# A graph layer whose sender rows come by indirect gather: one tile of 32 fetched row by row from two hardware queues

## The reference

```
h   = relu(layernorm(x))
s,v = h[:, :32] @ W_up_s, h[:, 32:] as [n, 32, 3] @ W_up_v      # the node table
w0..w3 = split(silu(silu(ef @ A1 + b1) @ A2 + b2) @ A3)          # per edge, ef has 8 features
ss, vs = s[src], v[src]                                         # one table row of 128 per edge
messages = [ss*y_s*w0, <vs,y_v>*w3/sqrt3, ss*y_v*w1, vs*y_s*w2] # 256 per edge
sums = segment_sum(messages, dst) / 10
out  = x + sums @ (W_out_s, W_out_v)
```

## Time and profile before

| | |
|---|---|
| profiled execution | 2015.58 us, span 2013.8 us |
| median of 3 runs | 2017.62 us |
| GpSimd busy | 1490.8 us (74%); 1563 gathers of 944 ns, 475.7 us of issue between them |
| TensorE busy | 1534.8 us (76%), mean granted clock 0.857 |
| VectorE busy | 977.2 us (49%) |
| ScalarE busy | 417.8 us (21%) |
| DMA engines | about 2 tenths busy in each slice, mean 64 GB/s |

### The profile page before, as it was taken

How to read it: one execution, slowest core, us unless ns; L and a number is a source line. 1 busy time by engine, 2 the same in 40 slices (tenths; PEclk the granted TensorE clock), 3 DMA queues, 4 the chain that set the end, 5 groups by cost and what they waited for, 6 DMA issues and landing times.

```text
span 2013.8 us, 47824 instructions
## 1 busy us (share of the span) xinstructions
PE 1534.8 (76%) x16198; PEld 936.5 (47%) x16198; DVE 977.2 (49%) x2232; ACT 417.8 (21%) x836; POOL 1490.8 (74%) x1627
## 2 busy tenths in 40 slices
PE   6877878778788787787787877777868777778685
PEld 3544545445444444454444444544545445444443
DVE  4444444444444444444444444444444444444444
ACT  4222222222222222222222222222222222212221
POOL 4777777777777777777777777777777777777774
PEclk8888898888978988879888888898898888988987
DMA  8222222222222222222222222222222222222222
GB/s 231 58 60 58 59 57 60 57 59 58 59 57 60 57 59 58 59 59 58 59 57 60 57 59 58 59 57 60 57 59 58 59 57 60 57 59 58 59 57 101
DMA packets 110964, 128.22 MB, mean 64 GB/s; under 512 B 70498, under 2 KB 83074, under 8 KB 110820
## 3 DMA queue, kind: packets, MB, share of 16 engines
q0 software_dynamic: 50336, 102.64, 18.1%
q1 hardware_dynamic: 60420, 25.36, 4.7%
q10 hardware_dynamic: 192, 0.02, 0.0%
HBM read 121.46 MB, written 6.43 MB: 64 GB/s over the span
## 4 chain that ended last, share of the span: by engine, by line
POOL 71%; issue 25%; POOLq 1%; PE 0%; DMA 0%; DVE 0%; SPq 0%; ACT 0%; DVEq 0%
POOL rows L520 71%; POOLq L515 1%; POOLq L517 0%; POOLq L525 0%; DMA rows<-node_table,src_in 0%; PE pss L740 0%; PE psw L718 0%; DMA src_in<-in_src 0%; PE psx L759 0%; DVE msgs L645 0%; SPq L475 0%; DVE xT_sb L661 0%; PE psx L751 0%; DVEq L653 0%; ACT sums_t L567 0%
## 5 line engine op out<-in xcount | busy, mean ns | idle before, releaser
L520 POOL DMA_INDIRECT rows<-node_table,src_in x1563 | 1474.9, 944 | 488.4 <-issue 475.7
L740 PE MATMUL pss<-msgs,onehot 128*32 128x64 f32 (+1 forms) x12544 | 333.6, 253 | 439.4 <-DVE msgs L645 437.6
L740 PEld LDWEIGHTS pss<-msgs,onehot 128*32 128x32 f32 x12544 | 262.2, 119 | 683.8 <-DVE msgs L645 674.5
L718 PE MATMUL psw<-a_bd,h 128*128 128x256 f32 x1568 | 560.7, 491 | 3.3 <-issue 0.2
L643 DVE TENSOR_TENSOR msgs<-rows,psw 128x256 f32<-128x256 f32 x392 | 165.2, 421 | 797.7 <-DMA rows<-node_table,src_in 779.6
L645 DVE TENSOR_TENSOR msgs<-rows,psw 128x768 f32<-128x768 f32 x392 | 371.2, 947 | 0.0
L718 PEld LDWEIGHTS psw<-a_bd,h 128*128 128x128 f32 x1568 | 324.2, 229 | 85.2 <-issue 25.3
L555 ACT ACTIVATE h<-ps,b_sb 128x512 f32<-128x512 f32 x196 | 134.7, 687 | 1014.2 <-PE ps L708 1014.2
L702 PE MATMUL ps<-ef_in,a_bd 16*128 16x512 f32 x392 | 238.4, 690 | 14.3 <-DMA ef_in<-in_efT 12.5
L708 PE MATMUL ps<-h,a_bd 128*128 128x512 f32 x392 | 246.8, 717 | 0.9 <-ACT h L555 0.9
L661 DVE TENSOR_TENSOR xT_sb<-xT_sb,psx 128x32 f32 x784 | 145.7, 186 | 199.8 <-DVE xT_sb L661 159.9
(11 more groups left out here) (60 smaller groups left out, 135.7 us busy)
## 6 DMA issues: line engine op xcount, KB each, us to landing
rows<-node_table,src_in POOLq DMA_INDIRECT x1563
ef_in<-in_efT SPq DMA_DIRECT2D x98, 64.0 KB
xT_sb<-in_xT SPq DMA_DIRECT2D x7, 448.0 KB, 8.4
x_sb<-in_x SPq DMA_DIRECT2D x7, 448.0 KB, 7.4
attr_in<-in_attr SPq DMA_DIRECT2D x98, 32.0 KB
out_T<-xT_sb SPq DMA_DIRECT2D x1, 3136.0 KB, 8.9
node_table<-tab_sb SPq DMA_DIRECT2D x7, 256.0 KB, 3.8
src_in<-in_src SPq DMA_DIRECT2D x98, 8.0 KB, 1.5
```

Of the source, the lines that this page charges most:

```text
L520: pool.indirect_dma_start(out=rows[:, QT * p + t, :], out_offset=None, in_=table, in_offset=bass.IndirectOffsetOnAxis(ap=src_in[:, b, at:a ...
L718: last = nc.tensor.matmul(psw[:, p % SLOTS, 2 * i:2 * i + 2].rearrange("p b c d e -> p (b c d e)"), h2[:, b, h, (2 * half + i) * P:(2 * ha ...
L740: last = nc.tensor.matmul(to, onehot[:, o, QT * half + w, c, :], moving, start=(half == 0 and c == 0), stop=(half == 1 and c == 3), skip_g ...
```

## The change

The last tile of each iteration (`SINGLE_SLOT`, slot 31, the fourth of quad 7) is no longer gathered by GpSimd, except in the last iteration. Its 128 senders come in a list of their own (`singles`, one row of 128 per iteration, built on the host from the same indices). SyncE loads the list for the iteration ahead, VectorE multiplies it by 128 to give element offsets (`row_at`), and SyncE (rows 0 to 71) and ScalarE (rows 72 to 127) each load the offsets into registers and issue one DMA of 512 B for every row. SyncE does 36 rows per block, in two lists of 18; ScalarE does 14 rows per oct, after `silu_2`. Both wait, before an iteration's first row, until the list is scaled and the messages of the iteration before are complete. `messages` of quad 7 waits for the rows of both engines beside its three gathers.

```diff
+SINGLE_SLOT = QT * QB - 1
+SP_ROWS = 72
+ACT_ROWS = P - SP_ROWS
+SP_PART = SP_ROWS // BODY
+ACT_PART = ACT_ROWS // (QB // 2)
...
+def quad_gathers(p):
+
+    return QT - 1 if QT * (p + 1) - 1 == SINGLE_SLOT else QT
...
+        table_flat = table.rearrange("n f -> (n f)").unsqueeze(0)
+
+        def row_starts(e, n, engine):
+            return nc.values_load_multi_w_load_instructions(
+                row_at[0:1, e:e + n], engines=[engine], min_val=0, max_val=(NPAD - 1) * F,
+                skip_runtime_bounds_check_because="the senders are node numbers")[1]
...
+                    def load_list(j):
+                        sp.dma_start(list_in[:, :], singles[bass.ds(j, 1), :]).then_inc(list_loaded, 16)
+
+                    def claim_singles(j):
+
+                        sp.wait_ge(list_scaled, j + 1)
+                        sp.sem_inc(sp_claimed, 1)
+                        sp.wait_ge(msgs_ready, j * QB + QB)
+                        sp.sem_inc(sp_claimed, 1)
+
+                    def gather_singles(b):
+
+                        for e0 in range(b * SP_PART, (b + 1) * SP_PART, SP_PART // 2):
+                            for i, at in enumerate(row_starts(e0, SP_PART // 2, mybir.EngineType.SP)):
+                                sp.dma_start(rows[e0 + i:e0 + i + 1, SINGLE_SLOT, :], table_flat[:, bass.ds(at, F)]
+                                             ).then_inc(sp_singles[b], 16)
+
+                    load_list(0)
...
                     with sp.Fori(0, NJ - 1) as j:
+                        claim_singles(j)
+                        load_list(j + 1)
                         for b in range(BODY):
-                            sp.wait_ge(gathered[b * QUADS + QUADS - 1], j * 16 * QT + 16 * QT)
+                            gather_singles(b)
+                            sp.wait_ge(gathered[b * QUADS + QUADS - 1],
+                                       j * 16 * quad_gathers(b * QUADS + QUADS - 1) + 16 * quad_gathers(b * QUADS + QUADS - 1))
                             load_src(j + 1, b)
...
                         for p in range(QB):
-                            gather(j, p)
+                            gather(j, p, quad_gathers(p))
...
+                    def gather_singles(o):
+
+                        e0 = SP_ROWS + o * ACT_PART
+                        for i, at in enumerate(row_starts(e0, ACT_PART, mybir.EngineType.Activation)):
+                            act.dma_start(rows[e0 + i:e0 + i + 1, SINGLE_SLOT, :], table_flat[:, bass.ds(at, F)]
+                                          ).then_inc(act_singles[o // 2], 16)
...
                             if not (last and o + 2 >= OCTS):
                                 silu_2(*ahead)
+                            if not last:
+                                if o == 0:
+                                    claim_singles(j)
+                                gather_singles(o)
...
+                    def scale_list(j):
+                        dve.wait_ge(list_loaded, j * 16 + 16)
+                        dve.tensor_scalar(row_at[:, :], list_in[:, :], float(F), None, ALU.mult).then_inc(list_scaled, 1)
...
+                        if singles:
+                            for b in range(BODY):
+                                dve.wait_ge(sp_singles[b], j * 16 * SP_PART + 16 * SP_PART)
+                                dve.wait_ge(act_singles[b], j * 16 * 2 * ACT_PART + 16 * 2 * ACT_PART)
...
+                            messages(j, p, quad_tiles(p) if last else quad_gathers(p), not last and quad_gathers(p) < QT)
+                            if not last and quad_gathers(p) < QT:
+                                scale_list(j + 1)
```

More of the change, by code:

```diff
@@ L84, in quad_tiles, with gnn_layer_kernel @@
     return sum(b < LAST_EDGES for b in begins)
-def gnn_layer_kernel(nc, x, xT, src, dst, dst_groups, attr, efT, Wus, Wuv, A1, b1, A2, b2, A3, Wos, Wov, outT):
+def quad_gathers(p):
+    return QT - 1 if QT * (p + 1) - 1 == SINGLE_SLOT else QT
+def gnn_layer_kernel(nc, x, xT, src, dst, dst_groups, singles, attr, efT, Wus, Wuv, A1, b1, A2, b2, A3, Wos, Wov, outT):
     table = nc.dram_tensor("node_table", (NPAD, F), F32, kind="Internal").ap()
@@ L147, in gnn_layer_kernel @@
         dst_in = sb("dst_in", [P, BODY, TILES], I32)
+        list_in = sb("list_in", [1, P], I32)
+        row_at = sb("row_at", [1, P], I32)
         src_in = sb("src_in", [P, BODY, TILES], I32)
@@ L200, in gnn_layer_kernel @@
         gathered = [sem(f"gathered{p}") for p in range(QB)]
+        list_loaded = sem("list_loaded")
+        list_scaled = sem("list_scaled")
+        sp_singles = [sem(f"sp_singles{b}") for b in range(BODY)]
+        act_singles = [sem(f"act_singles{b}") for b in range(BODY)]
+        sp_claimed = sem("sp_claimed")
+        act_claimed = sem("act_claimed")
         slots_claimed = sem("slots_claimed")
@@ L218, in gnn_layer_kernel @@
         out_stored = sem("out_stored")
-        round_sems = [round_step, *ef_loaded, *attr_loaded, *src_loaded, *gathered, slots_claimed, l1_done, h1_ready, l2_done,
+        round_sems = [round_step, *ef_loaded, *attr_loaded, *src_loaded, *gathered, list_loaded, list_scaled, *sp_singles, *act_singles, sp_claimed, act_claimed, slots_claimed, l1_done, h1_ready, l2_done,
                       h2_ready, w_ready, msgs_ready, rel_ready, eq_ready, onehot_ready, scatter_done, sums_copied, sums_turned, turned_copied, out_ready,
                       window_added]
+        table_flat = table.rearrange("n f -> (n f)").unsqueeze(0)
[3 more added lines that the diff above has]
+                skip_runtime_bounds_check_because="the senders are node numbers")[1]
         with nc.Block() as block:
@@ L497, in _ @@
                         load_attr(0, b)
+                    sp.wait_ge(table_stored, 16 * NCH * len(PIECES))
                     with sp.Fori(0, NJ - 1) as j:
+                        claim_singles(j)
+                        load_list(j + 1)
                         for b in range(BODY):
-                            sp.wait_ge(gathered[b * QUADS + QUADS - 1], j * 16 * QT + 16 * QT)
+                            gather_singles(b)
+                            sp.wait_ge(gathered[b * QUADS + QUADS - 1],
+                                       j * 16 * quad_gathers(b * QUADS + QUADS - 1) + 16 * quad_gathers(b * QUADS + QUADS - 1))
                             load_src(j + 1, b)
@@ L531, in _ @@
                     for p in range(QB):
-                        pool.wait_ge(gathered[p], (NJ - 1) * 16 * QT + 16 * quad_tiles(p))
+                        pool.wait_ge(gathered[p], (NJ - 1) * 16 * quad_gathers(p) + 16 * quad_tiles(p))
                     pool.dma_reset()
@@ L568, in copy_turned, with claim_singles @@
                                        ACT.Copy).then_inc(turned_copied, 1)
+                    def claim_singles(j):
+                        act.wait_ge(list_scaled, j + 1)
+                        act.sem_inc(act_claimed, 1)
+                        act.wait_ge(msgs_ready, j * QB + QB)
+                        act.sem_inc(act_claimed, 1)
+                    def gather_singles(o):
[3 more added lines that the diff above has]
+                                          ).then_inc(act_singles[o // 2], 16)
                     def iteration(j, first=False, last=False):
@@ L586, in _ @@
                         silu_2(0, o)
+                    act.wait_ge(table_stored, 16 * NCH * len(PIECES))
                     iteration(0, first=True)
@@ L633, in scale, with messages @@
                             ALU.mult).then_inc(onehot_ready, 1)
-                    def messages(j, p, tiles):
-                        dve.wait_ge(gathered[p], j * 16 * QT + 16 * tiles)
+                    def scale_list(j):
+                        dve.wait_ge(list_loaded, j * 16 + 16)
+                        dve.tensor_scalar(row_at[:, :], list_in[:, :], float(F), None, ALU.mult).then_inc(list_scaled, 1)
+                    def messages(j, p, tiles, singles):
+                        dve.wait_ge(gathered[p], j * 16 * quad_gathers(p) + 16 * tiles)
+                        if singles:
+                            for b in range(BODY):
+                                dve.wait_ge(sp_singles[b], j * 16 * SP_PART + 16 * SP_PART)
+                                dve.wait_ge(act_singles[b], j * 16 * 2 * ACT_PART + 16 * 2 * ACT_PART)
                         dve.wait_ge(w_ready, j * QB + p + 1 + W_CREDIT)
@@ L672, in iteration @@
                                     add_window(j, n + i)
-                            messages(j, p, quad_tiles(p) if last else QT)
+                            messages(j, p, quad_tiles(p) if last else quad_gathers(p), not last and quad_gathers(p) < QT)
+                            if not last and quad_gathers(p) < QT:
+                                scale_list(j + 1)
                             if ahead and p % 2 == 0:
@@ L678, in iteration @@
                                 scale(*ahead)
+                    scale_list(0)
                     relative(0, 0)
```

(4 more changed lines are left out.)

## The result

The changed kernel takes 3206.93 us (median of 4 runs, 3197.54 to 3207.56) against 2017.1 before: 1.5887 times as long, 95% interval 1.5868 to 1.5907. The forecast was 3225 us, so its total is 18 us off, 1.5% of the change; some of its parts are further off than that, and their errors cancel in part.

A forecast was written before the change was run, and what follows sets the result against it. GpSimd's gathers bound the kernel at 39.95 us per iteration; afterwards 4 x 7.9 + 4 x 6.9 + 5.9 = 65.1 us, +1207 us over 48 iterations, gives 3225 us. The range was 2740 to 3900 us.

The forecast's parts named there:

- The loop through ScalarE's 14 rows, copy_sums, turn and layer_2: Once per oct, ScalarE's rows delay copy_sums, hence TensorE's turn and layer_2, hence the next silu_2; 7.9 plus 6.9 us.
- The rival in which SyncE binds: ScalarE's rows fit its idle time and SyncE's own 47.6 us set the iteration: 2383 us, chance 7%.
- The dearer: Each row costs over a microsecond, by slow register loads or rows landing one after another: 5603 us, chance 7%.
- the faster rival: GpSimd still binds and the 60 us of dropped gathers are won: 1956 us, chance 3%.
- 14 rows and their list, four times: ScalarE's issue per oct: 14 rows at 0.45 us, 1.5 for the register list, 0.1 for waits; 7.9 us.
- the loop without them, four times: Per oct, copy_sums to turn 1.07 us and turn to silu_2 5.30; 6.4, up to 7.4 at lower clock, taken as 6.9.
- the iteration's edge, beyond these: Messages of quad 7 wait for the last rows: 4.9 us more before turn, 1.0 for quad 0's messages; 5.9 us.
- The upper end of 4048 us: The sum with 11.7 us for ScalarE's 14 rows and 7.4 for the rest of the loop, 82.3 us per iteration.
- a lower clock: TensorE, standing still some 7 us per oct, runs more of the loop at 1.2 GHz: 6.4 becomes up to 7.4 us.
- GpSimd was to wait for free slots: GpSimd's iteration needs only 38.7 us against 65.1 for the loop, so it waits for slots of `rows`.
- SyncE's loads behind 36 rows: SyncE's loads for the next iteration stand behind 36 rows each but are needed only an iteration later; costed at nothing.

## Why the prediction was right, step by step

**The cause.** The loop through ScalarE's 14 rows, copy_sums, turn and layer_2 was right, and is shown: ScalarE's rows alone give the whole loss, SyncE's alone 265 us, and moving ScalarE's rows out of the loop takes away 848 us. The rival in which SyncE binds is what is left once ScalarE fetches nothing (2282 us; its sum of 47.6 us per iteration measured 45.5). The dearer and the faster rival didn't come.

**The terms of the sum**, for the iteration of the timeline above.

| | predicted us | measured us | from |
|---|---|---|---|
| 14 rows and their list, four times | 31.6 | 32.6 | 8.92 + 7.30 + 8.82 + 7.51 |
| the loop without them, four times | 27.6 | 24.2 | 0.6 from copy_sums to turn + 5.4 from turn to silu_2 |
| the iteration's edge, beyond these | 5.9 | 8.1 | 1539.38 to 1553.54 less 6.05 |
| one iteration | 65.1 | 64.9 | |

The misses of +1.0, -3.4 and +2.2 us cancel to 0.2. That the total came so close is luck; that it lay in this loop is not. (The upper end of 4048 us in the sum lacks the 2.0 us that the forecast and the lower end have; it changes nothing.)

*The rows.* I had the issue too dear (14 rows in 5.45 to 5.56 us, 0.39 each instead of 0.45) and the list too cheap (2.3 us in the mean instead of 1.5). The two almost cancel. Taking VectorE's single load of 0.304 as the nearest row was poor guidance: a list isn't one load nor 14 of them, but 1.4 us or 3.2, by where it starts. The Trainium skill, page "Runtime: NRT & Kernel Launch", section "Instruction fetch mechanics", gives about 200 ns per register even in bulk, for loads from HBM. These loads from SBUF come near it where the list starts 8 bytes off: 3.19 us for 14 registers and 3.94 for 18 are 228 and 219 ns each. Where it is aligned they don't: 14 take 1.40 us, 100 ns each.

*The loop without them.* 1.07 us from copy_sums to turn at the run's end is 0.62 in the loop. The second part, 5.4, is near the 5.3 of the kernel before. I had added half a microsecond for a lower clock; in ordinary octs the lower level covers mostly scatter and layer_3 (1.30 and 2.08 us), as it did before (1.02 to 1.29 and 2.08).

*The edge.* This is the step that failed in its mechanism, within a right total. I had turn wait for VectorE's four window adds, and scatter behind it for the messages of quad 0. The timelines of VectorE and TensorE at the edge (all engines' start us, us):

```profile
1540.68 0.42 DVE L718 TENSOR_TENSOR msgs<-rows,psw 128x256 f32<-128x256 f32 x1 [20.38 <-DMA rows<-node_table]
1541.02 0.95 DVE L720 TENSOR_TENSOR msgs<-rows,psw 128x768 f32<-128x768 f32 x1
...
1544.73 0.19 DVE L736 TENSOR_TENSOR xT_sb<-xT_sb,psx 128x32 f32 x1 [0.45 <-DVE xT_sb L736]
1545.05 0.42 DVE L718 TENSOR_TENSOR msgs<-rows,psw 128x256 f32<-128x256 f32 x1
```

```profile
1542.02 1.30 PE L818 MATMUL pss<-msgs,onehot 128*32 128x128 f32 x32 [11.58 <-DVE msgs L720]
1543.25 2.07 PE L796 MATMUL psw<-a_bd,h 128*128 128x256 f32 x4
1545.25 2.07 PE L780 MATMUL ps<-ef_in,a_bd 16*128 16x512 f32 x2
1547.25 0.69 PE L829 MATMUL psx<-identity,sums 128*128 128x128 f32 x2
1547.87 1.29 PE L818 MATMUL pss<-msgs,onehot 128*32 128x128 f32 x32
```

The adds end at 1544.92, and the messages of quad 0 at 1546.34, both before turn. Turn starts as late as 1547.25 because TensorE, in its own order, does scatter, layer_3 and layer_1 first, each at the lower clock after 11.6 us of standing still. Two windows of 1 us show the two levels (the columns as in the earlier trace rows, the granted clock third from the right):

```profile
1546.00:1547.00 1.00, 1.00 (x2) 0.00 (x0) 0.96 (x4) 0.00 (x0) 0.21 (x1) 0.50 0.13 34
...
1554.00:1555.00 1.00, 1.00 (x13) 0.68 (x4) 0.89 (x3) 0.23 (x1) 0.00 (x0) 1.00 0.00 0
```

The same path stood in the trace before, at clock 1.00, ahead of the turn at 1017.55:

```profile
1014.71 0.76 PE L740 MATMUL pss<-msgs,onehot 128*32 128x128 f32 x32 [0.26 <-DVE msgs L645]
1016.46 1.12 PE L702 MATMUL ps<-ef_in,a_bd 16*128 16x512 f32 x2
```

There layer_1 and the adds (1017.49) ended within 0.1 us of each other, and I gave the 2.9 us from messages to turn to the adds alone. From scatter to turn TensorE took 2.84 us then and takes 5.23 at the lower clock. So from the last row's issue to turn it is 7.9 us, not 6.0. Behind turn I had 1.0 us more than in an ordinary oct, for a wait for messages; it is 0.9, but scatter doesn't wait there, and layer_2 takes 1.60 us instead of 1.02.

So I had the lower clock in the wrong place: in ordinary octs it adds little to what it cost before, and most at the edge. Messages were right (1.3 us), and they start 1.3 us after the last row's issue ends, where I had 1.5 for the landing.

**What should have shown.** GpSimd's gathers kept 0.944 us and its share fell to 45% (44% said). Ahead of turn TensorE stood 839 us in 145 waits for copy_sums, 5.8 us each, where I said about 7. That is three octs of each iteration; at the edge it stood ahead of the scatter of quad 7 instead (557 us in 50 waits for messages). SyncE's queue did wait for what VectorE does behind the messages of quad 7 (901 us, for the scaled list). GpSimd was to wait for free slots; the trace has it otherwise (us in total, times, longest):

```profile
POOL rows L568 <- DMA src_in<-in_src: 1046.8, 95, 19.5
...
POOL rows L568 <- DVE msgs L720: 233.6, 88, 7.4
```

I had costed SyncE's loads behind 36 rows at nothing. They do make GpSimd late, by up to 19.5 us at a time, but it has that much to spare; the run with ScalarE's rows alone shows that they cost nothing here.

## What to carry to other kernels

An engine's idle share says nothing of the price of new work on it: find the instruction behind which the work stands, who waits for the next one, and whether that comes back round. The same rows cost 1190 us behind silu_2 and 341 ahead of it. Of work given away count what the giver saves, here a whole gather's 1.25 us but 0.04 for half of one. Then count the rate that the other queue has to spare: SyncE kept pace with 64 rows per 40 us in aligned lists, and not with 72 in lists of which half were slow.

## What the runs showed of the hardware

A load of 14 registers from SBUF in one instruction took 1.40 us on ScalarE where the list began on a multiple of 16 bytes and 3.19 us where it began 8 bytes past one; of 18 on SyncE, 1.65 and 3.94 us; of 16 on SyncE, aligned, 1.23 us. Moving the lists removed the slow loads (ScalarE's median went from 2.29 to 1.40 us), so the start is the cause and not what ran beside them. Why 16 took less than 14 isn't shown.

An indirect gather of 64 rows on GpSimd took 0.90 to 0.91 us against 0.944 for 128. A DMA of one row whose address is in a register was issued by ScalarE in 0.231 us, one every 0.39 us; with an address fixed at build time every 0.30 us.
